# A state-space layer with a mixture of experts on one core: a chunk's own state moves into the bank of its output, the first routed expert's sums into a bank of their own, and VectorE's work of four slots is dealt out anew

## The reference, cut to what matters

```python
x = x + L0_attn(layernorm(x))       # scan layer
x = x + L0_ffn(layernorm(x))        # experts
# L0_attn: proj = rmsnorm(x) @ w_in  ->  z, x, B, C, dt;  x = silu(conv(x));  per head, chunk after chunk:
M     = exp(where(mask, lcs_l - lcs_i, -inf));   G = C B^T        # "gram", masked and weighted: mg
intra = (M * G) x ;   inter = exp(lcs) C h
h_new = exp(lcs_last) * h + sum_l M[last, l] x_l B_l             # state: decayed old one + the chunk's own
y     = intra + inter + D x ; out = residual + rmsnorm(y * silu(z)) @ w_out
# L0_ffn: two shared and four routed experts, F = 512; of the routed the two best, weighted by a softmax gate
relu(x @ w1 + b1) @ w2 + b2
```

## Time and profile before

| | |
|---|---|
| runs | 575.18, 575.23, 577.2 us; median 575.23 |
| the profiled execution | 571.37 us, span of its instructions 569.6 us |
| mean granted clock of TensorE | 0.996 |
| TensorE matmul busy | 541.9 us, 95% of the span |
| TensorE weight loads | 428.5 us, 75% |
| VectorE | 437.3 us, 77% |
| ScalarE | 355.9 us, 62% |
| GpSimd | 173.0 us, 30% |

### The profile page before, as it was taken

One profiled execution on the slowest core, in us unless ns is written; L12 is line 12 of the kernel. 1 busy time (PEld: TensorE's weight loads), 2 busy tenths in 40 slices (PEclk: granted clock), 3 DMA queues, 4 the chain that ended last, 5 costly groups with the idle time before them and its releaser, 6 DMA issues.

```text
span 569.6 us, 11656 instructions
## 1 busy us (share of the span) xinstructions
PE 541.9 (95%) x3912; PEld 428.5 (75%) x3912; DVE 437.3 (77%) x1037; ACT 355.9 (62%) x767; POOL 173.0 (30%) x232
## 2 busy tenths in 40 slices
PE   8887999999989999999999999999999999899996
PEld 7666778877877777877777777778777778777774
DVE  5868868978699777978778787987778777675654
ACT  4894579547675478636776387745886377752442
POOL 3074405520162203620155201622045211442011
PEclk9989999999999999999999999999999999999999
DMA  6650027200550006500371005600073004500030
GB/s 200 193 152 2 0 73 173 64 1 2 157 167 1 2 6 206 115 1 0 106 162 54 0 0 157 166 0 0 32 201 89 0 0 137 148 25 1 26 72 20
DMA packets 37353, 41.41 MB, mean 73 GB/s; under 512 B 3482, under 2 KB 27716, under 8 KB 37316
## 3 DMA queue, kind: packets, MB, share of 16 engines
q1 hardware_dynamic: 36724, 40.80, 26.1%
q10 hardware_dynamic: 592, 0.15, 0.1%
HBM read 37.79 MB, written 3.15 MB: 72 GB/s over the span
## 4 chain that ended last, share of the span: by engine, by line
PE 48%; DVE 20%; issue 9%; DMA 9%; ACT 8%; POOL 3%; SPq 2%; DVEq 0%; ACTq 0%; POOLq 0%
PE bank L425 7%; DMA grow<-lc_rows 6%; PE bank L427 5%; PE bank L426 5%; PE bank L534 4%; PE bank L639 4%; DVE cv L1122 4%; PE bank L640 4%; PE bank L641 4%; ACT act_h L871 3%; DVE act_l L1269 3%; PE bank L546 2%; PE bank L562 2%; ACT L968 2%; PE bank L556 2%
## 5 line engine op out<-in xcount | busy, mean ns | idle before, releaser
L1269 DVE SCALAR_TENSOR_TENSOR act_l<-bank,act_h 128x512 fp32r<-128x512 f32 x192 | 131.7, 687 | 66.2 <-ACT act_h L871 64.1
L871 ACT ACTIVATE act_h<-bank 128x512 fp32r<-128x512 f32 x192 | 114.3, 596 | 79.4 <-PE bank L427 75.7
L1493 POOL TENSOR_TENSOR late<-late 128x512 f32<-128x512 f32 x31 | 39.8, 1285 | 166.3 <-DVE late L1277 165.7
L425 PE MATMUL bank<-fTl,w1h 128*128 128x512 f32 x192 | 86.9, 452 | 1.2 <-DVE act_l L1269 0.5
L891 ACT ACTIVATE seg<-seg,lneg 128x128 f32<-128x128 f32 x256 | 81.2, 391 | 3.7 <-DMA seg<-lc_rows 3.7
L639 PE MATMUL bank<-act_l,w2h 128*128 128x512 f32 x192 | 77.6, 404 | 1.5 <-DVE act_l L1269 1.5
L640 PE MATMUL bank<-act_h,w2l 128*128 128x512 f32 x192 | 76.0, 396 | 0.0
L427 PE MATMUL bank<-fTh,w1h 128*128 128x512 f32 x192 | 75.7, 394 | 0.0
L641 PE MATMUL bank<-act_h,w2h 128*128 128x512 f32 x192 | 75.6, 394 | 0.0
L426 PE MATMUL bank<-fTh,w1l 128*128 128x512 f32 x192 | 75.5, 393 | 0.0
L1480 POOL TENSOR_TENSOR xw<-xs,seg 128x128 f32<-128x128 f32 x48 | 20.0, 416 | 153.0 <-ACT seg L891 87.5
(11 more groups left out here) (176 smaller groups left out, 1059.3 us busy)
## 6 DMA issues: line engine op xcount, KB each, us to landing
seg<-lc_rows SPq DMA_DIRECT2D x32, 512.0 KB, 4.2
late<-gk_rows SPq DMA_DIRECT2D x8, 1024.0 KB, 9.1
grow<-lc_rows SPq DMA_DIRECT2D x48, 128.0 KB, 4.8
x_in<-L_attn_hidden_dram SPq DMA_DIRECT2D x8, 256.0 KB, 4.1
out_dram<-late SPq DMA_DIRECT2D x8, 256.0 KB, 3.7
late<-L_ffn_sw_dram SPq DMA_DIRECT2D x2, 512.0 KB, 7.2
late<-L_ffn_rw_dram SPq DMA_DIRECT2D x1, 1024.0 KB, 7.7
CT<-L_attn_w_in_proj_dram SPq DMA_DIRECT2D x1, 512.0 KB, 5.4
```

Of the source, the lines that this page charges most:

```text
L425: mm(dst, stat_h, mov_l, start=True, stop=False)
L871: nc.scalar.activation(act_h[:, b % RING, :], HID[b % 2][:], ACT.Relu).then_inc(act_h_ready, 1)
L1269: v_.scalar_tensor_tensor(act_l[:, r, :], HID[b % 2][:], 0.0, f(act_h[:, r, :]), ALU.max, ALU.subtract)\
```

## The change

- `state_product` is split off from `y_product` and moved one slot earlier, to step 1 (slots 13, 16, 19). It writes the unused half (columns 256 to 511) of `MAIN[0]`, the bank of y, and waits for the y of the chunk before to be read.
- `y_product(s, c)` begins with a wait for the state of chunk c itself (before: of chunk c-1), then issues `gram` of chunk c+1, then y.
- On VectorE, in bodies 1 to 7: the state of a chunk (`next_state`) moves from slots 14, 17, 20 to 13, 16, 19, behind `act_low`. The two halves of `mg` for chunks 1 and 2 move to slots 15 and 18, one ahead of `act_low`, one behind; for chunk 3 both to slot 21. The statistics of `norm1` stay ahead of `act_low` in slot 15, the rest of it and `norm1_apply` go behind it.
- `sum_bank`: blocks 8 to 11 sum in `MAIN[1]`, except in the last sequence. The waits in `second` stay as they were.
- The third `b_copy` moves from ScalarE (end of slot 5) to VectorE (slot 5, ahead of `act_low`), with a semaphore of its own.
- `growth` of chunk 1 moves on ScalarE from slot 12 to the end of slot 14's scan work. SyncE issues the rows for chunk 1 (`segments`, `growth_rows`) ahead of the output store, where they stood behind it and its wait.
- GpSimd waits for `hn_ready` in slot 18, before `add_term`.

```diff
         def sum_bank(s, b):
 
-            return MAIN[3] if is_seq(s, n_seq - 1) and (b < 8 or b // 4 in (3, 5)) else FOUT
+            if is_seq(s, n_seq - 1):
+                return MAIN[3] if b < 8 or b // 4 in (3, 5) else FOUT
+            return MAIN[1] if b // 4 == 2 else FOUT
...
                     segments(s, 0)
+                    segments(s, 1)
+                    growth_rows(s, 1)
                 if older is not None:
                     sp_eng.wait_ge(out_ready, nth(older, 1, 1))
                     sp_eng.dma_start(out_dram[older], out_t).then_inc(out_stored, 16)
                 if s is not None:
-                    segments(s, 1)
-                    growth_rows(s, 1)
                     growth_rows(s, 2)
...
-            def y_product(s, c):
-
+            def state_product(s, c):
                 if c > 0:
                     pe.wait_ge(state_step, nth(s, 8, (2, 5, 8)[c - 1]))
+                    pe.wait_ge(y_steps, nth(s, 8, 2 * c))
+                pe.wait_ge(btok_ready, nth(s, 3, c + 1))
+                pe.wait_ge(xw_ready, nth(s, 6, 2 * c + 2))
+                for n in range(NP):
...
+                ins.then_inc(s_psum, 1)
+
+            def y_product(s, c):
+
+                pe.wait_ge(state_step, nth(s, 8, (2, 5, 8, 8)[c]))
                 if c < NCH - 1:
-                    pe.wait_ge(btok_ready, nth(s, 3, c + 1))
-                    pe.wait_ge(xw_ready, nth(s, 6, 2 * c + 2))
-                    for n in range(NP):
...
+                    gram(s, c + 1, None)
                 if c > 0:
                     pe.wait_ge(y_steps, nth(s, 8, 2 * c))
...
-                    if b == 0:
+                    if b == 0 and c == NCH - 1:
                         pe.wait_ge(mg_ready, nth(s, 8, 2 * c + 2))
...
-                    if step == 1:
+                    if step == 1 and c == 0:
                         gram(s, c, prev)
-                        if c == NCH - 1 and not is_seq(s, n_seq - 1):
-                            proj(s + 1, 0)
+                    if step == 1 and c < NCH - 1:
+                        state_product(s, c)
+                    if step == 1 and c == NCH - 1 and not is_seq(s, n_seq - 1):
+                        proj(s + 1, 0)
...
-                        if c < NCH - 2:
-                            growth(s, c + 1)
+                        if c == 1:
+                            growth(s, 2)
...
+                    if step == 2 and c == 0:
+                        growth(s, 1)
...
-                    if s is not None and i == 5:
-                        b_copy(s, 2)
...
+            def third_b_copy(s):
+                dve.wait_ge(proj_psum, made(s, 8))
+                v_.tensor_copy(BT[:, 2, :], MAIN[0][:]).then_inc(b_third_ready, 1)
...
+                if step == 1 and (c == 0 or is_seq(s, 0)):
+                    masked_gram(s, c, 0)
+                    masked_gram(s, c, 1)
...
+                    if c < NCH - 1 and is_seq(s, 0):
+                        next_state(s, c)
                     dve.wait_ge(y_psum, nth(s, 4, c + 1))
...
+                own = MAIN[0][:, 256:512].rearrange("p (n d) -> p n d", n=NP)
...
+                        if i in (15, 18, 21):
+                            masked_gram(s, i // 3 - 4, 0)
+                        if i == 15 and not is_seq(s, n_seq - 1):
+                            norm1_stats(s + 1)
+                        if i == 21:
+                            masked_gram(s, 3, 1)
...
+                    if s is not None and i == 5:
+                        third_b_copy(s)
                     if prev is not None and i in (15 + LAG, 19 + LAG):
                         routed_out(prev, (i - 15 - LAG) // 4)
                     if (new := block_at(i, prev, older)) and not (i == 0 and prev is not None):
                         act_low(*new)
                     if older is not None and i == (7 if s is not None or prev is None else 9):
                         store(older)
+                    if s is not None and i in (15, 18):
+                        masked_gram(s, i // 3 - 4, 1)
+                    if s is not None and i in (13, 16, 19):
+                        next_state(s, i // 3 - 4)
+                    if s is not None and i == 15 and not is_seq(s, n_seq - 1):
+                        norm1(s + 1)
+                    if s is not None and i == 18 and not is_seq(s, n_seq - 1):
+                        norm1_apply(s + 1)
...
+                    if prev is not None and s is not None and i == 16 + LAG and not last:
+                        pool.wait_ge(hn_ready, nth(s + 1, 4, 4))
```

More of the change, by code:

```diff
@@ L458, in proj @@
                     pe.wait_ge(y_steps, v)
-                if j == 0 and (v := nth(s, 8, 0)) is not None:
-                    pe.wait_ge(state_step, v)
+                if j == 0 and (v := nth(s, 4, -7)) is not None:
+                    pe.wait_ge(term_ready, v)
                 if j == 2 and (v := nth(s, 4, 0)) is not None:
@@ L782, in opening @@
                         b_tokens(0, c, None, None)
-                    gram(0, c, None)
+                    if c == 0:
+                        gram(0, c, None)
                     if c < 2:
@@ L790, in opening @@
                         proj(1, 0)
+                    if c < NCH - 1:
+                        state_product(0, c)
                     y_product(0, c)
@@ L838, in b_copy @@
                 act.wait_ge(proj_psum, made(s, b + 6))
-                nc.scalar.copy(BT[:, b, :], MAIN[(b + 2) % 4][:]).then_inc(b_ready, 1)
+                nc.scalar.copy(BT[:, b, :], MAIN[(b + 2) % 4][:]).then_inc(b_third_ready if b == 2 else b_ready, 1)
             def c_copy(s, b):
@@ L1084, in norm1 @@
                     v_.bn_stats(st1[:, c, :], x_in[:, c, :]).then_inc(ln1_stats, 1)
+            def norm1(s):
                 dve.wait_ge(ln1_stats, nth(s, 4, 4))
@@ L1183, in attend, with next_state @@
                     v_.tensor_tensor(yT[:, :, at(c)], yT[:, :, at(c)], szT[:, :, at(c)], ALU.mult).then_inc(yz_ready, 1)
+            def next_state(s, c):
+                first = (0, 2, 5)[c]
+                if c > 0:
+                    dve.wait_ge(grow_ready, nth(s, 3, c))
+                    v_.tensor_tensor(state_m[:], state[:, (c - 1) % 2], grow[:, c % 2, :, P - 1:P].to_broadcast([P, NP, 2 * HD]),
+                                     ALU.mult).then_inc(state_step, 1)
+                    dve.wait_ge(state_step, nth(s, 8, first + 1))
+                    first += 1
+                dve.wait_ge(s_psum, nth(s, 3, c + 1))
+                own = MAIN[0][:, 256:512].rearrange("p (n d) -> p n d", n=NP)
+                for t in range(2):
+                    q, d = slice(64 * t, 64 * t + 64), slice(HD * t, HD * t + HD)
+                    if c == 0:
+                        v_.tensor_copy(state[q, c % 2, :, d], own[q, :, d]).then_inc(state_step, 1)
+                    else:
+                        v_.tensor_tensor(state[q, c % 2, :, d], own[q, :, d], state_m[q, :, d], ALU.add).then_inc(state_step, 1)
+                dve.wait_ge(state_step, nth(s, 8, first + 2))
             def mean_square(s):
@@ L1303, in scan_part @@
                     attend(s, *divmod(i - CHUNKS_FROM, 3))
-                if i == 15 and not last:
-                    norm1(s + 1)
-                if i == 18 and not last:
-                    norm1_apply(s + 1)
             def body(s, prev, older):
@@ L1399, in opening @@
                     scan_part(0, i)
+                    if i == 15:
+                        norm1_stats(1)
+                        norm1(1)
+                    if i == 18:
+                        norm1_apply(1)
                     if i == NBLK - 4:
```

50 lines of the change are left out of this document (17 added, 33 removed).

## The result

| | before | after |
|---|---|---|
| median of the runs | 576.22 us (4 runs, 575.18 to 581.14) | 625.29 us (4 runs, 620.77 to 626.82) |
| ratio | | 1.0851, interval 1.0796 to 1.0906 |
| the profiled execution, its span | 571.37, 569.6 us | 624.40, 622.7 us |
| mean granted clock of TensorE | 0.996 | 0.970 |

The change makes the kernel 8.5% slower. The forecast had the sign, the place and the kind of the stall; of +49.1 us it had +26.1, and its range ended at 613.

What follows compares the result with a forecast made beforehand. TensorE, busy 95% of the span, was taken to bound the kernel, so new stalls are paid nearly in full. 33.3 - 5.6 - 3.1 - 1.5 + 3.0 = +26.1 us on 575.2 gave 601.3; own range 595 to 608, wider 594 to 613.

Steps and rivals of the forecast that it cites:

- The new wait: TensorE behind `second` waits for the same chunk's state: 1.38 us in chunk 0, 1.84 in chunks 1 and 2; net +33.3 us.
- GpSimd's wait for `hn_ready`: Delays an addition whose reader comes three slots later, while `norm1_apply` runs undisturbed: 0.
- Rival A: TensorE's clock falls as well at the new stalls: one fall a body makes +12, 613 us; chance 0.17.
- The old wait on `mg`: y's separate wait for `mg` goes, 5.6 of 6.6 us being in the bodies: -5.6 us.
- The third copy of B: On VectorE, it ends TensorE's 0.44 us a body before a projection: -3.1 us, the other end being 0.
- One group fewer: `gram` of chunk 3 joins y of chunk 2, one fp32 matmul group fewer, 0.21 us a body: -1.5 us.
- The bank of the first expert: Waits at blocks 8 and 12 stay; the projection waiting for this expert's term does so five slots later: 0.
- slot 21: Both `mg` halves ahead of `routed_out` stall `second` up to 0.4 us a body, about as much returned: 0, bad end 3.
- The opening: TensorE now waits for the state before y and issues `gram` between: 0 to 6.0 us, middle taken, +3.0.
- C: Rival: the stall does not show, VectorE's state being ready when `second` ends; gains alone stand, 565.0 us; chance 0.03.
- D: Rival: the state wait is short and costs half, 17 us instead of 33: 585 us; chance 0.04.
- B: Rival: exponentials ahead of `relu`, or `norm1_apply` ahead of `act_low`, 0.5 us late in chunks 1 and 2: 608 us; chance 0.08.

Runs made afterwards that it cites:

- the fillers: Changed kernel with useless matmuls ahead of the state wait: 616.51 us with 4, 6 and 9 in chunks 0 to 2, 613.09 us with chunks 1 and 2 only.
- both gains: Kernel before with third copy of B on VectorE, `growth` of chunk 1 in slot 14 and its rows ahead of the output store: 567.59 us, 0.9852.

## Why the prediction was wrong in size

Two terms that the sum put at nothing were real: the clock (11.2 us) and GpSimd's wait (6.4 us). Without the one the kernel took 613.09, without the other 618.87, both still above the forecast's own 595 to 608; no run at the shared bank leaves out both.

*The new wait, +33.3.* Right in place, count and mechanism: 21 stalls in the bodies, 1.29 in chunk 0 (forecast 1.28) and about 1.80 in chunk 1 (1.74). Wrong in chunk 2, where "`state_m`, 0.45 to the next start" took its duration from a place where no large GpSimd operation ran beside it. Measured: 39.8.

*GpSimd's wait for `hn_ready`, 0.* This step failed, and it is what lengthened chunk 2. "It delays an addition whose reader comes three slots later" was true, and asked only who waits for the addition, not what it now runs beside. "In return `norm1_apply` runs undisturbed" bought nothing: its four operations take 1.11, and 1.11 without the wait too. The addition, let go at their end, meets `state_m`, on which TensorE's next start hangs. Price: 6.4 us, of which the stalls of chunk 2 are 18.2 - 13.7 = 4.5.

*The clock, a rival instead of a term.* This is the largest step that failed: the sum has nothing for it. Rival A set one fall a body at +12, with a chance of 0.17; the run had 27.3 us at half clock in the bodies, against A's 7 x 3.4 = 23.8, and the fillers price them at 11.2 to 12.2. So A's size was right, in part by luck: it had seven falls at 1.7 us each, and there were eight times 3.4 us at 1.4 each. Its time of 613 was not right, since the other failed terms are not in it. The evidence lay in the opening, where no single idle time had been long; the argument against it, that the matmuls around the stalls are wide and dense, did not hold for stalls of about two microseconds. The section "HAM oscillation — how this bites in real kernels" of the Trainium skill's page "TensorE: Matmul & The Clock Gate" lets the clock fall only behind long idle gaps and would have the time without these 11 to 12 us; the trace disagrees, with half clock behind an idle time of 1.77 us and within one of 2.74. The micro-idles of its section "A second HAM failure mode: psum-queue depth-cycling" are nearer to it.

*The old wait on `mg`, -5.6.* Right: alone it gave 6.0 in the bodies, and 8.7 by the medians.

*The third copy of B, -3.1.* Failed. "VectorE's copy needs 0.60 us of an idle stretch (VectorE is 23% idle)" took an average over the span for a stretch in which VectorE is the last to be ready. Measured: 0, and by itself slightly below nothing.

*One group fewer, -1.5.* Not seen. The bodies with own bank and without GpSimd's wait, which have one group fewer and the copy, sum to 454.1, against 453.8 with `growth` alone. No run did it by itself, so it stays open.

*The bank of the first expert, and slot 21: 0.* The first does not show in the waits of the changed kernel, and no run has it alone. Of the second a little shows: `second` waits for `routed_out` in three bodies, 0.9 us in all, where up to 0.4 a body was feared.

*The opening, +3.0.* Measured +6.7, but a part is chance: with the opening's code unchanged or nearly so it took 56.69, 57.02, 58.47 and 60.74 us in four profiled executions (before, `growth`, both gains, copy of B), with one to three stretches at half clock. With the changed opening it took 61.6 to 64.9 in five. The means are 58.2 and 63.1, so +4.9 is the fairer number. With the new order but the state's own bank it took 59.0 and 59.7, so most of it is the wait for the state, which in the changed kernel's opening reaches 3.7 us.

*The sum.* In the profiled spans 53.1 - 26.1 = 27.0 us were missing: 11.2 of clock in the bodies, 6.5 of longer stalls (39.8 - 33.3), 5.1 of gains that did not come (-5.1 for -10.2), 3.7 in the opening and 0.4 in the rest, together 26.9. The medians differ by 4 less, since the execution of before that was profiled lies 4.9 us under its median, and its opening, the shortest of all those above, may explain part of that.

*The rivals.* C and D fell as argued. B's late `relu` or `act_low` did not come: both stand within 0.1 us of their clean distances. Whether the wait could be left out at the shared bank was not tried.

## What to carry to other kernels

Before giving two chains one bank, write down the longest trip (TensorE, ScalarE, VectorE and back) that the first must now wait for, and add the clock: here stalls of 1.3 to 2.8 us, three a body, cost 39.8 us, and the clock more than a quarter of that on top. Take an operation's duration from a place with the same neighbours, and ask of every delayed operation what it will run beside, not only who waits for it. An idle share of an engine says nothing of the slot; look which engine is last there.

## What the runs showed of the hardware

- **Two VectorE operations with both inputs in SBUF ended 0.29 us after the GpSimd operation beside them.** `state_m` took 1.27 us beside an addition of GpSimd and 0.41 without it; with the state's own bank the product with silu(z) took 1.42 beside `CTe`. The Trainium skill, page "SBUF — State Buffer", section "Who interferes with whom", says that a VectorE instruction with two SBUF inputs contends with a GpSimd instruction that reads SBUF. The trace agrees: `state_m` ends at 408.02, 0.29 after the addition (407.73).
- **Half clock came in bodies with an idle time of about two microseconds.** In the changed kernel it came in five of seven bodies, five times at the stall of chunk 2 (idle 1.86 to 2.76 us) and once behind that of chunk 1 (1.77). Three times it set in within the idle time, three times 0.5 to 1.3 us behind it. Without GpSimd's wait it came at idle times of 1.70 to 1.92, with the shared bank alone at 1.70 to 2.77, with the copy of B alone at 1.83 and 1.99. In no body whose longest idle time was 1.55 or less (before, the state ahead of `act_low`, own bank) did it come. Nor did it always come behind a long one: two bodies of the changed kernel with 2.43 and 2.75 had none.
- **The same opening varied by 3.3 us from one execution to another.** Five kernels here share the code of the changed opening; it took 61.63, 62.89, 62.90, 63.35 and 64.88 us, and the shortest had 6.8 us at half clock, the longest 14.3. A single profiled execution is that uncertain here.
